# The one-hot buffers of an edge loop: two in turn, addressed by a register, where one was shared

## What is computed

```python
agg = jax.ops.segment_sum(h[src], dst, num_segments=N)
...
exp_e = jnp.exp(weighting_gate - m)
row_sum = jax.ops.segment_sum(exp_e, src, num_segments=n_nodes)
out0 = jax.ops.segment_sum(atten_e[:, None] * Mfeat[dst], src, num_segments=n_nodes)
out1 = jax.ops.segment_sum(atten_e[:, None] * Mfeat[src], dst, num_segments=n_nodes)
```

## Time and profile before

| what | us |
|---|---|
| median of 3 runs | 1561.6 |
| lowest, highest | 1560.73, 1564.66 |
| the profiled execution | 1564.89 |
| its span | 1563.2 |
| PE busy in the span | 1436.4 |
| DVE busy in the span | 1022.6 |
| the edge loop, first to last visit (about) | 67 to 314 |

### The profile page before, as it was taken

How to read it: one execution, slowest core, us unless ns; L and a number is a source line. 1 busy time by engine, 2 the same in 40 slices (tenths; PEclk the granted TensorE clock), 3 DMA queues, 4 the chain that set the end, 5 groups by cost and what they waited for, 6 DMA issues and landing times.

```text
span 1563.2 us, 24236 instructions
## 1 busy us (share of the span) xinstructions
PE 1436.4 (92%) x9089; PEld 1196.2 (77%) x9089; DVE 1022.6 (65%) x1824; ACT 484.5 (31%) x911; POOL 331.2 (21%) x206
## 2 busy tenths in 40 slices
PE   3898988888999999999999899999899999989998
PEld 2787877776776877787788688877787879768887
DVE  5978778879984485249625666676725473665786
ACT  2623111132241121013012432433432430453675
POOL 1000002144303003100300113113111302303687
PEclk9999999899999999999999899999999999998999
DMA  5213223342232002001100100101000095526843
GB/s 154 88 54 96 94 95 146 122 158 80 85 114 85 1 0 74 28 0 66 62 27 1 54 28 27 55 28 55 27 28 28 28 221 133 210 72 187 230 82 49
DMA packets 52285, 123.96 MB, mean 79 GB/s; under 512 B 8561, under 2 KB 28936, under 8 KB 45038
## 3 DMA queue, kind: packets, MB, share of 16 engines
q1 hardware_dynamic: 19200, 74.15, 14.4%
q10 hardware_dynamic: 23117, 38.00, 7.6%
q0 software_dynamic: 9856, 10.28, 3.7%
HBM read 92.87 MB, written 40.22 MB: 85 GB/s over the span
## 4 chain that ended last, share of the span: by engine, by line
PE 75%; DVE 12%; issue 4%; ACT 4%; DMA 2%; POOL 1%; DVEq 1%; ACTq 0%; SPq 0%; PEldq 0%; PEld 0%; POOLq 0%
PE ps L649 9%; PE ps L650 9%; PE ps L651 9%; PE ps L2302 8%; PE ps L707 4%; PE ps L709 4%; PE ps L660 4%; PE ps L661 4%; PE ps L662 4%; PE ps L985 2%; PE ps L3110 2%; DMA rows<-d_xg,BC 2%; PE ps L2205 2%; DVE XL L1478 1%; PE ps L2207 1%
## 5 line engine op out<-in xcount | busy, mean ns | idle before, releaser
L649 PE MATMUL ps<-wslot,XH 128*125 128x512 f32 (+1 forms) x520 | 202.2, 389 | 7.9 <-DVE XL L1478 6.2
L651 PE MATMUL ps<-wslot,XL 128*125 128x512 f32 (+1 forms) x520 | 200.6, 386 | 0.0
L650 PE MATMUL ps<-wslot,XH 128*125 128x512 f32 (+1 forms) x520 | 200.5, 386 | 0.0
L2992 POOL CAST wslot<-arena 128x2048 fp32r<-128x2048 f32 x25 | 47.6, 1906 | 711.4 <-PEq L3078 354.5
L660 PE MATMUL ps<-XH,wslot 128*128 128x500 f32 (+1 forms) x336 | 123.6, 368 | 15.3 <-DVE XL L1478 8.2
L661 PE MATMUL ps<-XH,wslot 128*128 128x500 f32 (+1 forms) x336 | 122.6, 365 | 0.0
L649 PEld LDWEIGHTS ps<-wslot,XH 128*125 128x125 f32 x520 | 96.5, 185 | 33.4 <-DVE XL L1478 7.5
L707 PE MATMUL ps<-CTr,Hhi 125*128 125x500 f32 (+1 forms) x360 | 121.8, 352 | 0.0
L662 PE MATMUL ps<-XL,wslot 128*128 128x500 f32 (+1 forms) x336 | 121.8, 362 | 0.0
L1483 DVE TENSOR_TENSOR arena<-ps,arena 125x512 f32<-125x512 f32 x140 | 91.4, 684 | 44.1 <-PE ps L651 43.5
L2302 PE MATMUL ps<-arena 125*128 x1330 | 93.8, 224 | 27.3 <-DVE arena L2591 23.7
(11 more groups left out here) (468 smaller groups left out, 3182.3 us busy)
## 6 DMA issues: line engine op xcount, KB each, us to landing
arena<-in_units SPq DMA_DIRECT2D x29, 1024.0 KB, 4.8
arena<-in_units SPq DMA_DIRECT2D x8, 2048.0 KB, 8.3
d_w<-arena ACTq DMA_DIRECT2D x10, 625.0 KB
d_wt<-arena ACTq DMA_DIRECT2D x10, 625.0 KB, 4.9
rows<-in_rows ACTq DMA_DIRECT2D x22, 256.0 KB, 4.1
d_kv<-V SPq DMA_DIRECT2D x20, 250.0 KB
arena<-d_kv SPq DMA_DIRECT2D x20, 250.0 KB
arena<-d_wt ACTq DMA_DIRECT2D x2, 2187.5 KB
```

The lines of the kernel that those rows point to most:

```text
L649: pe.matmul(o, lhsT=xh[:, k, s], rhs=H4[:, k, 0:nw], start=k == 0, stop=False, skip_group_check=True)
L650: pe.matmul(o, lhsT=xh[:, k, s], rhs=L4[:, k, 0:nw], start=False, stop=False, skip_group_check=True)
L651: last = pe.matmul(o, lhsT=xl[:, k, s], rhs=H4[:, k, 0:nw], start=False, stop=k == K - 1, skip_group_check=True)
```

## The change

The buffer list `more` is gone. Its memory and another stretch 1450 words (`more_step`) behind it, which holds values that are no longer used once the loop runs, are seen as one flat array `more_flat`, and a register `more_place` on PE and on DVE, which an exclusive or turns between 0 and 2900 (bf16 elements) after each visit of the loop, says where the one-hot stands. DVE starts with a credit of two in `more_used` in place of one.

```diff
--- before.py
+++ after.py
@@ -416,13 +416,17 @@
         oh = [gr(NT * 64, TP).bitcast(BF16), gr(NT * 64, TP).bitcast(BF16),
               rows[0:TP, 3:5, :].rearrange("p s d -> p (s d)")[:, 0:NT * 64].bitcast(BF16),
               BC[0:TP, 1, 526:526 + NT * 64].bitcast(BF16)]
-        more = [gr(NT * 64, TP).bitcast(BF16) for _ in range(MORE)]
+        more_at = _g[0]
+        gr(NT * 64, TP)
         iota_s = gr(NT * 64).bitcast(I16)
         srcx = gr(NCP, TP)
         dlow = gr(NCH, TP).bitcast(BF16).rearrange("p (c two) -> p c two", two=2)
         exw = gr(NCH, TP)
         hbf = [gr(NCH, TP).bitcast(BF16).rearrange("p (c two) -> p c two", two=2) for _ in range(2)]
         assert _g[0] <= AT_ZERO
+        more_step = NT * 64 + NT * 64 + NCP
+        more_flat = arena[0:TP, more_at:more_at + more_step + NT * 64].bitcast(BF16)
+        assert more_at + more_step + NT * 64 <= _g[0]
         dstf = V[0:TP, 1, 176:176 + NCH]
         ew = BC[0:TP, 0, 0:NCH]
         srcf = BC[0:TP, 0, 176:176 + NCH]
@@ -2258,6 +2262,8 @@
             pe.wait_ge(pre_ready, 1)
             mores = pe.alloc_register("pe_mores")
             pe.reg_mov(mores, 0)
+            more_place = pe.alloc_register("pe_more_place")
+            pe.reg_mov(more_place, 0)
 
             def turn_part(g, i, b):
                 q = 3 * g + i
@@ -2308,10 +2314,15 @@
                     pe.wait_ge(oh_ready, VIS * b + i + 1)
                     visit(oh[i], lo + i, i == 0).then_inc(oh_used, 1)
                 with pe.Fori(lo + VIS, hi, MORE) as c:
-                    for i in range(MORE):
-                        pe.wait_ge(more_ready, pe.snap(mores) + 1)
-                        visit(more[i], c + i, False).then_inc(more_used, 1)
-                        pe.reg_add(mores, mores, 1)
+                    pe.wait_ge(more_ready, pe.snap(mores) + 1)
+                    place = pe.snap(more_place, min_val=0, max_val=2 * more_step)
+                    for t in range(NT):
+                        last = pe.matmul(ps[:, 3 * (b % 2) + t // 4, 128 * (t % 4):128 * (t % 4) + 128],
+                                         lhsT=more_flat[:, bass.ds(place + 128 * t, 128)],
+                                         rhs=pre_flat[:, bass.ds(c * 128, 128)], start=False, stop=False, skip_group_check=True)
+                    last.then_inc(more_used, 1)
+                    pe.reg_alu(more_place, more_place, 2 * more_step, ALU.bitwise_xor)
+                    pe.reg_add(mores, mores, 1)
                 pe.drain().then_inc(blk_full, 1)
                 if b in IN_LOOP:
                     kind, t = IN_LOOP[b]
@@ -2441,7 +2452,7 @@
             settle()
             own(dve.tensor_copy(blkf, blki))
             settle()
-            dve.sem_inc(more_used, MORE)
+            dve.sem_inc(more_used, 2)
             dve.wait_ge(bounds_ready, 1)
             own(dve.scalar_tensor_tensor(srcx[:, 0:NCH], blkf, float(BLK), srcf, ALU.mult, ALU.add))
             own(dve.scalar_tensor_tensor(dlow, blkf.unsqueeze(2).to_broadcast([TP, NCH, 2]), -float(BW),
@@ -2586,6 +2597,8 @@
             q_out(6)
             dve.sem_inc(pre_ready, 1)
             dve.reg_mov(mores, 0)
+            more_place = dve.alloc_register("dve_more_place")
+            dve.reg_mov(more_place, 0)
 
             def one_hot(buffer, c, b):
                 return dve.tensor_scalar(buffer, iota_s[0:TP, :], srcx[:, bass.ds(c, 1)], -float(BLK * b),
@@ -2624,10 +2637,11 @@
                         dve.wait_ge(oh_used, VIS * (b - 1) + i + 1)
                         one_hot(oh[i], lo + i, b).then_inc(oh_ready, 1)
                 with dve.Fori(lo + VIS, hi, MORE) as c:
-                    for i in range(MORE):
-                        dve.wait_ge(more_used, dve.snap(mores) + 1)
-                        one_hot(more[i], c + i, b).then_inc(more_ready, 1)
-                        dve.reg_add(mores, mores, 1)
+                    dve.wait_ge(more_used, dve.snap(mores) + 1)
+                    place = dve.snap(more_place, min_val=0, max_val=2 * more_step)
+                    one_hot(more_flat[:, bass.ds(place, NT * 128)], c, b).then_inc(more_ready, 1)
+                    dve.reg_alu(more_place, more_place, 2 * more_step, ALU.bitwise_xor)
+                    dve.reg_add(mores, mores, 1)
                 if b in (1, 14, 26):
                     unit_low({1: 1, 14: 2, 26: 3}[b])
                 if b - 1 in IN_LOOP:
```

## The result

The changed kernel takes 1582.1 us (median of 4 runs, 1579.0 to 1587.0) where the kernel before takes 1562.2 (4 runs, 1560.7 to 1564.7): ratio 1.012, 95% interval 1.010 to 1.014, so **19.8 us slower**, outside the predicted range of 1553 to 1575. Its profiled execution is the fastest of its four: 1579.0 us, span 1577.3, 14.1 us longer than that of before.

What follows compares the result with a forecast made beforehand. PE was taken to bound the early edge loop, with DVE often setting the pace in the late one. Register work +15.5 us and -13.3 coming back gave +2.2 on the median 1561.6: 1563.8 us, no change, range 1553 to 1575.

Steps and rivals of the forecast that it cites:

- The pace and the lead: PE's loop visits: 0.13 us per matmul with its register operation, sequencer only 0.7 us ahead of the engine.
- The rival drawn from the Trainium skill: PE's queue, 64 deep, hides all register work in loop visits, so nothing is added: 1535 us, chance 0.06.
- +15.5 us of register work: PE's edge loop: 0.31 us for each of 27 blocks with one loop visit, 0.55 for 13 with two.
- 0.33 us for the operation, the counters and the branch: PE's sequencer after a loop visit's tenth matmul: ALU operation, counters and branch take 0.33 us with their gaps.
- the unit wait of 1.4 us: PE's wait for a weight unit's low half, 1.4 us, goes because DVE's stop right before it goes.
- -13.3 us that come back: Edge loop: 7.8 us of late block starts, 1.4 of weight unit wait and 4.1 of slow clock go.
- the late block starts of 228.48, 233.41 and 241.07: PE's waits at block starts behind DVE's late work go: 1.2, 1.1 and 2.2 us of the 7.8 priced.
- the 2.6 us priced for it: Block start at 303.70: without idle time the clock stays up and the slow matmuls give back 2.6 us.
- 13.3 + 13.3 = 26.6: PE's waits for DVE's second one-hot in 13 blocks, 13.3 us, plus the 13.3 us that come back.
- what is late next: Late loop: DMA loads of keys and values, for which POOL waits, start some 3 us later; no term in the sum.
- The DMA rival: Late loop: loads or the group's store keep block starts late, only some 5 us come back: +10, 1572 us, chance 0.10.
- The dear operation: PE's sequencer in 53 loop visits: 0.15 us per matmul, deciding from about 0.136: +12, 1573 us, chance 0.22.

Runs made afterwards that it cites:

- experiment 1: The changed kernel with the register kept but not turned and one credit, so one shared buffer addressed through the register: 1589.2 us, ratio 1.015.
- experiment 5: Two buffers at fixed addresses (fifth visit written out, later ones in a conditional loop) plus two-part d_w stores, against the kernel before: 1539.8 us, ratio 0.985.
- experiment 9: The kernel of experiment 5 with one buffer instead of two, the sixth one-hot taking the fifth's: 1564.2 us, ratio 1.001 to the kernel before.
- Experiment 3: The changed kernel with each store of d_w issued in two parts, rows 0 to 111 and 112 to 124: 1572.5 us, ratio 1.006.
- experiment 6: The changed kernel with the loads of keys and values in two parts and the d_w stores whole: 1574.3 us, ratio 1.006.
- experiment 7: The kernel before with one plain register operation behind each of the ten matmuls of a loop visit, addresses fixed: 1572.5 us, ratio 1.006.

## Why the prediction was wrong

**The pace and the lead: right.** 0.13 us was forecast for each matmul, 0.125 measured: 46 ns for the operation where 47 was taken, and 0.08 for the gap and the handing over, as estimated (0.06 and 0.02). The lead of 0.7 us held as well: the fifth visit's last matmuls already starve. The rival drawn from the Trainium skill, page TensorE: Matmul & The Clock Gate, table at its head (a queue of 64), is not borne out as a cover for this work; here the lead before the change was 0.7 us, some 12 matmuls, and 1.3 us of issue did not fit behind it: the fifth visits' last matmuls are 0.124 us apart.

**+15.5 us of register work: a little small.** Among the blocks with a dense product, one with one loop visit lost 0.23 to 0.41 us, 0.31 in the mean of ten, just as forecast; one with two lost 0.71 to 0.81, 0.75 in the mean of five, instead of 0.55. That makes 27 x 0.31 + 13 x 0.75 = 18.1. The second visit starts after 0.66 us of idle time. What the sum had too small there is the branch back: its 0.33 us for the operation, the counters and the branch has room only for the median of L2310, 67 ns, and that is the branch when it does not go back. In both kernels 40 of the 53 took 0.06 to 0.11 us and the other 13, which go back for a second visit, 0.21 us and more (0.235 in block 3 after the change). Before the change this lay in the time in which PE waited for DVE's one-hot anyway.

What the sum left out is the clock: with matmuls issued one by one PE's granted clock fell in the early loop too, to 0.98 in this profile, 0.96 and 0.94 in experiment 1, where all profiles without an operation for each matmul have 1.00. In this profile it ate the unit wait of 1.4 us that was to come back: behind block 14 the time from the last visit's last matmul to the dense row is down from 1.59 to 0.66 us, and the first seven dense matmuls then take 3.1 us, at the lower level of the clock. That these falls come from the slow visits rests on five profiles with such operations (0.94 to 0.98 in one or both windows) against six without (1.00 in all twelve), and on their place: the five profiles have 14 falls before 221 us, and all 14 come 0.1 to 1.8 us after the last matmul of a block with two loop visits. Idle time alone does not do it, since the kernel before has 0.86 us of it in the same blocks and keeps its clock. No run was made to show it by itself.

**-13.3 us that come back: the step that failed.** The waits of DVE for PE went as forecast, and so did the late block starts of 228.48, 233.41 and 241.07: 0.99, 0.18 and 0.12 us of idle PE where 2.10, 1.10 and 2.22 were. The start at 303.70 has 0.12 us for 2.01 too, but the clock fell there all the same for 3.4 us (321.1 to 324.5), so the 2.6 us priced for it came back in part at most. With fixed addresses and split stores (experiments 5 and 9) the second buffer brings 24.4 us, against 13.3 + 13.3 = 26.6 in the prediction. The mechanism and its size were right. The step that failed is the sum's last one, what the forecast made of "what is late next": nothing. It named the later start of the loads, and left out a price for it; the wait for a store went into a rival at 0.10, in which "only some 5 us come back" of 13.3, a cost of 8.3 us. Experiment 3 puts it at 9.6. So that rival had the cause and nearly the size, but not the way: the old late starts did go, and new ones, of 4 and 5 us with half clock behind them, came where before stood 0.61 and 1.86. The row that could have told was there: read_block of block 32 waited 1.16 us for a store under way since 250.07, for 30 us, while the five stores without loads beside them had taken 9 to 12. Such a store has no slack, and the prediction argued against the rival that DVE is held there only once. It asked when the loads start and not what they do to the store that shares their engines. For group 5 it was the order that turned: 3 us ahead of the loads before, 1.3 us behind them now.

In the terms of the account above: the second buffer -24.4 where 26.6 were forecast, the registers +32.7 where the forecast had 2.2 + 26.6 = 28.8, the stores +9.6 where it had 0. These are 2.2, 3.9 and 9.6 us too little, 15.7 of the 17.6 by which the forecast missed the 19.8. The profiled executions differ by 14.1 us only; three of the changed kernel's four runs took 3 to 8 us more than its profiled one, and no trace shows where they lost it.

**The signs.** The chance of slower stood at 0.38, below same at 0.42. The dear operation (0.22) named the right side for a wrong reason: 0.136 us per matmul was not reached. The DMA rival (0.10) had the right mechanism, at 1572; the result lies 10 us beyond, and the larger register work and the clock are what the runs offer for that.

**From which version to go on.** Two buffers at fixed addresses with split stores (experiment 5) takes 1539.8 us, 1.5% less than the kernel before. The idea of the change was worth it; its form of addressing cost more than it brought.

## What to carry to other kernels

An address from a register is not free where PE runs short matmuls: in this kernel each such operation cost its own time and 0.08 us more on the sequencer, against a pace of 0.056 us, so PE starved as soon as the lead of 0.7 us was used up. Two buffers can be had without it: write the common case out with a fixed address and keep the loop, with the other fixed address, for the rare one (experiment 5). And when you price a branch from its row, take the taken ones by themselves; a median over all can hide them.

When an edit takes away an engine's stop, ask for each thing it will now reach earlier how long that had been under way: a wait of 1 us at the end of a 30 us transfer is a warning, not a small cost. A DMA whose outer dimension is 125 loads few engines, which shows as a share of 0.3 at 123 GB/s; cut 112 + 13 it landed in time.

## What was not expected of the hardware

A store of 625 KB that takes 9 to 12 us by itself took 16 to 39 us beside loads of the same row count, though the DMA engines were on average 0.3 busy; and the same bytes split by rows, or the loads split by rows, ended that (experiments 3 and 6). A register operation of 32 ns between two matmuls sets them 0.112 us apart, one of 46 ns 0.125 (experiment 7 and the changed kernel). A branch that goes back took 0.21 us and more on PE's sequencer where one that falls through took 0.067. And slow visits seem to take the clock from the work behind them: dense matmuls at the lower level for 3.4 us, though PE had been idle for no more than 0.66 us at a time before them. The 14 falls all stand in such a place, but no run separates the cause.
